# Gated cross-attention and expert layer: query rows made and turned earlier in a block, a written-out prologue order, and W_qv loaded from ScalarE's queue

## The reference, cut to what matters

```python
x = x + tanh(g_x) * xattn(layernorm(x), ctx)          # x: 4096 x 512, ctx: 3202 x 512
x = x + tanh(g_f) * moe(layernorm(x))                 # 8 experts, top 2, 512 -> 2048 -> 512, gelu

def xattn(e, c):
    Sim = (e @ w1)[:, None] + (c @ w2)[None, :] + (e * w3) @ c.T + b
    hq = softmax(Sim, axis=1) @ c                     # each row of x looks at all of ctx
    hc = softmax(max(Sim, axis=1)) @ e                # one pooled row for all of x
    return concat([e, hq, e * hq, e * hc]) @ W_qv + b_qv
```

## Time and profile before

| | |
|---|---|
| median of 3 runs | 2383.6 us |
| the profiled execution | 2384.36 us |
| its span | 2382.6 us |
| granted TensorE clock, mean | 0.967 |
| TensorE busy | 2215.5 us (93%) |
| VectorE, ScalarE busy | 1304.1 us (55%), 1146.8 us (48%) |
| share of the chain of waits: TensorE, VectorE, DMA | 82%, 5%, 4% |

### The profile page before, as it was taken

How to read it: one execution, slowest core, us unless ns; L and a number is a source line. 1 busy time by engine, 2 the same in 40 slices (tenths; PEclk the granted TensorE clock), 3 DMA queues, 4 the chain that set the end, 5 groups by cost and what they waited for, 6 DMA issues and landing times.

```text
span 2382.6 us, 34706 instructions
## 1 busy us (share of the span) xinstructions
PE 2215.5 (93%) x12045; PEld 1134.6 (48%) x12045; DVE 1304.1 (55%) x2667; ACT 1146.8 (48%) x1749; POOL 143.9 (6%) x141
## 2 busy tenths in 40 slices
PE   4799999999999999999899998599999999999997
PEld 2344444444444444444444544365564656556463
DVE  5556555555554555554366677556464555646450
ACT  4655555455555455554453334354463635446360
POOL 0000000000000000000002221201011010101101
PEclk8999999999999999999999999799999999999999
DMA  6444433444443344433578774433334353333421
GB/s 186 100 95 103 97 98 75 96 100 103 94 97 77 95 101 95 100 82 77 136 223 221 214 193 124 117 100 88 101 88 110 140 129 97 93 101 88 115 75 22
DMA packets 480081, 264.81 MB, mean 111 GB/s; under 512 B 419380, under 2 KB 419508, under 8 KB 475948
## 3 DMA queue, kind: packets, MB, share of 16 engines
q1 hardware_dynamic: 469164, 243.85, 38.4%
q0 software_dynamic: 10880, 20.52, 4.5%
HBM read 97.96 MB, written 71.52 MB: 71 GB/s over the span
## 4 chain that ended last, share of the span: by engine, by line
PE 82%; DVE 5%; DMA 4%; ACT 3%; issue 2%; SPq 1%; another core or an unknown queue 1%; POOL 1%; DVEq 0%; POOLq 0%; ACTq 0%
PE ps L1178 22%; PE ps L1194 19%; PE ps L1828 18%; PE ps L1843 17%; PE ps L1578 4%; DMA arena<-arena 3%; DMA rows<-arena 1%; SPq L526 1%; PE ps L364 1%; ACT arena L1047 1%; DVE arena L766 1%; ACT arena L1026 1%; ACT arena L1036 0%; ACT arena L995 0%
## 5 line engine op out<-in xcount | busy, mean ns | idle before, releaser
L1178 PE MATMUL ps<-arena 128*128 128x512 f16 (+1 forms) x2688 | 591.1, 373 | 64.2 <-DMA arena<-arena 61.1
L1194 PE MATMUL ps<-arena 128*128 128x512 f16 x2400 | 557.4, 381 | 0.0
L1828 PE MATMUL ps<-arena 128*128 128x320 f16 x3072 | 420.1, 300 | 17.3 <-DMA arena<-rows 17.3
L1178 PEld LDWEIGHTS ps<-arena 128*128 128x128 f16 x2688 | 257.0, 101 | 369.3 <-issue 108.1
L1843 PE MATMUL ps<-arena 128*128 128x512 f16 x1920 | 415.7, 379 | 0.0
L1026 ACT ACTIVATE arena<-ps,arena 128x512 f32<-128x512 f32 (+1 forms) x224 | 163.8, 732 | 499.1 <-PE ps L1178 499.1
L1194 PEld LDWEIGHTS ps<-arena 128*128 128x128 f16 x2400 | 235.5, 99 | 282.1 <-issue 11.8
L1828 PEld LDWEIGHTS ps<-arena 128*128 128x128 f16 x3072 | 301.1, 98 | 136.1 <-issue 17.4
L753 DVE TENSOR_REDUCE arena<-arena 128x1 f32<-128x512 f32 (+1 forms) x224 | 140.3, 626 | 312.1 <-ACT arena L1026 311.4
L1843 PEld LDWEIGHTS ps<-arena 128*128 128x128 f16 x1920 | 187.9, 98 | 225.3
L766 DVE SCALAR_TENSOR_TENSOR arena<-arena 128x512 f16<-128x512 f32 x192 | 144.1, 750 | 184.2 <-ACT arena L1047 184.2
(11 more groups left out here) (230 smaller groups left out, 1380.5 us busy)
## 6 DMA issues: line engine op xcount, KB each, us to landing
arena<-in_L_ffn_w SPq DMA_DIRECT2D x64, 1024.0 KB, 9.9
feats<-arena SPq DMA_DIRECT2D x48, 512.0 KB, 2.8
arena<-in_x SPq DMA_DIRECT2D x32, 512.0 KB, 3.6
rows<-arena SPq DMA_DIRECT2D x13, 774.0 KB, 3.8
out<-arena SPq DMA_DIRECT2D x16, 512.0 KB, 2.9
arena<-in_ctx SPq DMA_DIRECT2D x6, 1024.0 KB, 13.2
arena<-arena SPq DMA_TRANSPOSE x272, 3.1
arena<-in_L_xattn_W_qv SPq DMA_DIRECT2D x4, 1024.0 KB, 10.1
```

The source lines that it names most:

```text
L1178: mm = pe.matmul(out, qT[:, q, s * KD + k, :], ctxT[:, r * KD + k, a:z], start=(k == 0 and s + r == 0), stop=(k == KD - 1 and s == 1))
L1194: mm = pe.matmul(psO[q], turned, ctxN[:, j, r, :], start=(j + s + r == 0), stop=False)
L1828: mm = pe.matmul(psH[:, f % 2, h, :], w1s[:, s, k * F + f * P:k * F + (f + 1) * P], XT[:, r, k, h * HALF:(h + 1) * HALF], start=(k + s + r ...
```

## The change

The query rows of both units of the next block are made at steps 0 and 3 of the second half, their high parts at steps 1 and 4, their low parts at steps 2 and 5. SyncE turns the even one behind the fourth transpose of P. In the prologue the loop over t is gone and each engine has its order written out. Context tiles 0 to 3 are turned by TensorE and the other 22 by DMA; VectorE makes all four copies of turned tiles. `FIRST[q][c]` is the place of unit q's chunk c in the common order of the first 14 score groups. The low part and the pooling weight of a block's normalised rows have semaphores of their own, and those of block 1 are made in `half(1, 0)`. At the hand-over ScalarE issues the four loads of W_qv, one behind each of the probabilities 0 to 3 of unit 31; all four sums stand at step 0 of the last half; and SyncE loads the first features and rows of x for the merge right behind the transposes of unit 31, ahead of the store of unit 30.

The diff, cut to its core; the long orders of the prologue are given as lists.

```diff
-    def load_weights(self, sp):
-        for n in range(4):
-            (the four W_qv parts, on sp)
+    def load_weights(self, eng, n):
+        (part n alone, on eng)
...
-    LAG = 3
-    BY_PE = list(range(2 * TC))
+    FIRST = ((0, 1, 2, 3, 5, 7, 8), (4, 6, 9, 10, 11, 12, 13))
-    LK = 5 * QT + 2
+    LK, EK = 3 * QT + 1, QT + 1
-    UNIT0 = LAG + 2 * (LAST - LAG) + 1
+    UNIT0 = FIRST[0][LAST] + 1
+    psQ = ps[:, 3, :].bitcast(F16).rearrange("p (k i) -> p k i", i=P)
...
 sync, body:
+                if c == 2 and first:
+                    store_e(1)
+            if last:
+                load_first()
             for c in range(NC):
                 if not last:
                     turn_p(u, c)
+                if c == 3 and norms:
+                    turn_q(u + 2, 0)
                 if c == 4:
                     store_f(u - 2, 0)
-                if c == 5 and norms:
-                    turn_q(u + 2, 0)
+        def load_first():
+            sp.wait_ge(qk_done, NC * U)
+            sp.wait_ge(e_out, 16 * NB)
+            for v in range(2):
+                sp.wait_ge(f_out[v], 16 * (U // 2))
+            mg.load_feats(sp, feats, 0, 0)
+            mg.load_x(sp, x, 0, 0)
+            sp.wait_ge(p_ready, NC * U)
+            mg.load_feats(sp, feats, 1, 1)
+            mg.load_x(sp, x, 1, 1)
 sync, prologue:
+        for j in range(TC, JT):
+            turn_ctx(j)
+        load_x(2)
         turn_q(2, 0)
+        store_e(0)
         for c in range(NC):
             turn_p(0, c)
-        store_e(1)
+        mg.load_small(sp)
         turn_q(3, 1)
 sync, end (the waits and loads that load_first() now has are gone from behind body(NB)):
-        sp.wait_ge(qk_done, NC * U)
-        mg.load_weights(sp)
+        sp.wait_ge(rows_blank, 16 * (NB - 2))
         body(NB, last=True, norms=False, loads=False)
...
 vector, half:
+                if norms and i and c in (2, 5):
+                    query_lo(2 * b + 2 + c // 3, c // 3, row0)
                 if c == 1 and not (first and not i):
                     outputs(u - 3, b - 1 if i else b + XR - 2, old)
...
-                if norms and i:
-                    if c in (2, 4):
-                        query_rows(2 * b + 2 + q, b + 1, q, row0, 0)
-                    if c in (3, 5):
-                        query_lo(2 * b + 2 + q, q, row0)
+                if first and not i:
+                    if c == 0:
+                        norm_lo(1)
+                    if c == 1:
+                        norm_weight(1)
+                if norms and i and c in (0, 3):
+                    query_rows(2 * b + 2 + c // 3, b + 1, c // 3, row0, 0)
...
 vector, prologue, in its new order (";" for a new line):
+ query_rows(0, 0, 0, ..); query_rows(0, 0, 1, ..); chunk_scale(0); ident; chunk_scale(1); split_low(0); split_low(1)
+ split_low(2); chunk_scale(2); turned(0); split_low(3); query_lo(0, ..); turned(1); split_low(4); turned(2)
+ chunk_scale(3); split_low(5); turned(3); split_low(6); split_low(7); chunk_scale(4); query_lo(1, ..); split_low(8)
+ split_low(9); chunk_scale(5); chunk_max(0, 0, 0); copy of qT[:, 1]; split_low(10); split_low(11); chunk_max(1, 0, 1)
+ chunk_scale(6); norm_stats(1); chunk_max(2, 0, 2); split_low(12); norm(1); query_rows(2, ..); common_scale()
+ chunk_max(3, 0, 3); query_lo(2, ..); chunk_max(4, 1, 0); norm_lo(0); chunk_max(5, 0, 4); (6, 1, 1); (7, 0, 5); (8, 0, 6)
+ row_max(0, ..); low(0, 0, 0); chunk_max(9, 1, 2); low(0, 0, 1); chunk_max(10, 1, 3); low(0, 0, 2); chunk_max(11, 1, 4)
+ low(0, 0, 3); query_rows(3, ..); chunk_max(12, 1, 5); low(0, 0, 4); chunk_max(13, 1, 6); row_max(1, ..); low(0, 0, 5)
+ query_lo(3, ..); low(0, 0, 6); norm_weight(0); pool_top(0, ..); tail_low(); value_scale(); pool_rows(0, ..)
 scalar, half:
-                if norms and i and c in (3, 5):
-                    query_high(2 * b + 2 + q, q, row0, RK * (2 * b + 2 + q) + 2)
+                if norms and i and c in (1, 4):
+                    query_high(2 * b + 2 + c // 3, c // 3, row0, RK * (2 * b + 2 + c // 3) + 2)
+                if last and not i and c < 4:
+                    if c == 0:
+                        act.wait_ge(qk_done, NC * U)
+                    mg.load_weights(act, c)
-                if last and i and c < 4:
-                    mg.sum_part(act, c)
+                if last and i and c == 0:
+                    for n in range(4):
+                        mg.sum_part(act, n)
+                if first and not i and c == 0:
+                    norm_hi(1)
 scalar, prologue, in its new order (scores(n) is the evacuation of the n-th group):
+ squares(0); query_high(0, ..); squares(1); split_high(0); squares(2); split_high(1); (2); (3); squares(3)
+ split_high(4); (5); squares(4); copy of qT[:, 0]; split_high(6); (7); squares(5); query_high(1, ..); scores(0)
+ split_high(8); (9); squares(6); scores(1); split_high(10); (11); scores(2); norm_sd(1); scores(3); split_high(12)
+ scores(4); query_high(2, ..); scores(5); scores(6); norm_hi(0); scores(7); scores(8); scores(9); wait common
+ probabilities 0, 1; scores(10); probabilities 2; scores(11); 3; scores(12); 4; scores(13); 5; query_high(3, ..); 6; pool_weight(0)
 tensor, prologue, in its new order (first_scores(q, c) waits for ct_turned[c] and the bank, then scores):
+ sums(0); sums(1); sums(2); turn(0); turn(1); sums(3); turn(2); turn_query(0, psQ); turn(3); sums(4); wait q0_ready, ct_out
+ first_scores(0, 0); (0, 1); sums(5); (0, 2); turn_query(1, psT[0]); sums(6); (0, 3); (1, 0); (0, 4); (1, 1); (0, 5); (0, 6)
+ (1, 2); (1, 3); wait common, g_step; psV; (1, 4); (1, 5); (1, 6)
```

More of the change, by code:

```diff
@@ L951, in vector @@
[L951 to L963 removed]
+        split_low(2)
+        chunk_scale(2)
@@ new lines, in vector @@
+        turned(0)
+        split_low(3)
+        query_lo(0, 0, rowbuf[0])
+        turned(1)
+        split_low(4)
+        turned(2)
+        chunk_scale(3)
+        split_low(5)
+        turned(3)
+        split_low(6)
+        split_low(7)
+        chunk_scale(4)
+        query_lo(1, 1, rowbuf[1])
+        split_low(8)
+        split_low(9)
+        chunk_scale(5)
+        chunk_max(FIRST[0][0], 0, 0)
+        dve.wait_ge(q0_done, 2)
+        dve.tensor_copy(qT[:, 1], psT[0]).then_inc(q0_ready, 1)
@@ L1130, in scalar @@
-        act.wait_ge(common, 4)
-        for c in range(NC):
-            probabilities(0, 0, c)
-            if c == 0:
-                query_high(3, 1, row0, RK * 3 + 2)
-            if c + LAST - LAG + 1 < NC:
-                n = UNIT0 + 1 + c
-                scores(n, n % 4, 1, c + LAST - LAG + 1)
-            if c == 1:
-                pool_weight(0)
+        squares(1)
+        split_high(0)
+        squares(2)
+        split_high(1)
+        split_high(2)
+        split_high(3)
+        squares(3)
@@ new lines, in scalar @@
+        split_high(4)
+        split_high(5)
+        squares(4)
+        act.wait_ge(q0_done, 1)
+        act.copy(qT[:, 0], psQ).then_inc(q0_ready, 1)
+        split_high(6)
+        split_high(7)
+        squares(5)
+        query_high(1, 1, rowbuf[1], 4)
+        scores(FIRST[0][0], 0, 0, 0)
+        split_high(8)
+        split_high(9)
+        squares(6)
+        scores(FIRST[0][1], 1, 0, 1)
+        split_high(10)
+        split_high(11)
+        scores(FIRST[0][2], 2, 0, 2)
+        norm_sd(1)
@@ L1140, in scalar @@
+        scores(FIRST[1][4], 3, 1, 4)
+        probabilities(0, 0, 3)
+        scores(FIRST[1][5], 0, 1, 5)
+        probabilities(0, 0, 4)
+        scores(FIRST[1][6], 1, 1, 6)
+        probabilities(0, 0, 5)
+        query_high(3, 1, row0, RK * 3 + 2)
+        probabilities(0, 0, 6)
+        pool_weight(0)
         half(1, 0, first=True)
@@ L1252, in tensor @@
         pe.matmul(psV, vmax.broadcast_to([P, P]), identf, start=True, stop=True).then_inc(v_done, 1)
-        for c in range(LAST - LAG + 1, NC):
-            n = UNIT0 + c - LAG
-            pe.wait_ge(scores_ready, n - 3)
-            scores(n % 4, 1, c)
+        first_scores(1, 4)
+        first_scores(1, 5)
+        first_scores(1, 6)
         half(1, 0, first=True)
```

270 lines of the change are left out of this document (114 added, 156 removed).

## The result

The changed kernel takes 2266.64 us (median of 4 runs, 2265.27 to 2268.44) against 2383.43 us (4 runs, 2383.19 to 2384.3) of the kernel before on the same chip: a ratio of 0.951, 95% interval 0.9493 to 0.9526. The forecast was 2259.0, in a range of 2248 to 2280. The table shows one step that is 9.1 us off, the hand-over, and all others within 1.1 us.

What follows compares the result with a forecast made beforehand. TensorE was taken as busy nearly everywhere, with room only in prologue, blocks and hand-over; gains of 29, 88.1 and 7.5 us, 124.6 in all, took the profiled 2384.36 us to 2259.8, as median 2259.0, range 2248 to 2280.

Steps and rivals of the forecast that it cites:

- Part 1: Blocks: query rows at step 0, even tile turned at step 3, closes TensorE's hole at each block border; 88.1 us.
- C: Block border: the hole closes but a next wait of 1 to 2 us shows; 2280 us, chance 0.07.
- D: Blocks: query row not ready by step 3, SyncE stands at it, 88.1 us stay; 2347 us, chance 0.03.
- E: Blocks: without rests TensorE is granted the low clock for part of them, so slower; 2560 us, chance 0.02.
- Part 2: Prologue: squares and splits up to three groups ahead of the scores break a one-behind-the-other chain; 29 us.
- The walk: Prologue: new engine orders stepped forward with old durations; steady start at 71 to 73 us instead of 103.7.
- Part 3: Hand-over to the merge: W_qv loads from ScalarE's queue let P's transposes land in 5 to 8 us; 7.5 us.
- sign of being wrong: Hand-over: a merge that starts 48 us after the last scores, as before the change.
- Rival A: Hand-over: W_qv's packets take the transposes' place on the DMA engines, only issue time gained, 2.4 us; 2264.1 us, chance 0.2.
- the sum: Whole kernel: gains of 88.1, 29 and 7.5 us off the profiled execution's 2384.36 us give 2259.8 us.

Runs made afterwards that it cites:

- e1: Changed kernel with the even query tile's transpose back behind P's sixth transpose, rows still made at steps 0 and 3: 2353.27 us.
- e2: Changed kernel with the query rows made at their old steps, the even tile's transpose still behind P's fourth: 2263.62 us.
- e8: Kernel before, with TensorE's sums in the prologue's loop moved behind the first score group of each step: 2376.84 us.
- e12: Kernel before, with the prologue's scales, squares, sums and splits one chunk further ahead and sums behind scores: 2367.36 us.
- e7: Changed kernel with norm_sd(1) behind split_high(12) and the thirteenth evacuation ahead of the fourth probability on ScalarE in the prologue: 2266.62 us.
- e10: Changed kernel run once more, nothing changed: 2261.5 us.
- e3: Changed kernel with the four W_qv loads on SyncE's queue ahead of the last unit's transposes of P, as before the change: 2262.0 us.
- e11: Changed kernel with all four W_qv loads issued by ScalarE at once behind probability 0: 2259.35 us.
- after: First run of the changed kernel as it stands, against the kernel before: 2266.64 us, ratio 0.951.
- e5: Changed kernel with the W_qv loads on SyncE's queue behind all seven transposes of the last unit: 2267.81 us.
- e6: Changed kernel with one W_qv load on SyncE behind each of the last unit's transposes 1 to 4, sums between the last probabilities: 2261.5 us.

## Why the prediction was right, and where it was not

**Part 1 was right in size and mechanism.** 88.0 us for 88.1, blocks at clock 1.00. By e1, 89.8 us are lost again when one DMA goes back to its old place in SyncE's order. What I had put beside it as its condition, the row made at step 0, is none (e2): the row at step 2 was early enough. Rivals C and D, a next wait at the border or a row too late, are not there, and E, the lower clock, neither.

**Part 2 was right in size:** 30.0 us for 29. The walk said that half (1,0) would start at 71.3, and it started at 72.21, with the slow first group that it allowed for. That squares, splits and sums ran one behind the other was a part of the cause: breaking it in one place gives 8.1 us (e8), looking ahead in all three gives half (e12), and where the other half comes from is open. Two things were read or argued wrongly. The period of 10.75 us does not hold for each chunk: the groups of scores start at 44.55, 55.30 and 66.05, and from there on TensorE has two and more groups in a row. And the walk has a stall of 4 us at norm_sd(1) on the way; moving it, together with one evacuation, gained nothing that can be told from the spread of the other runs (e7). So the 30.0 us agree with the walk's 29 better than its account of them does.

**Part 3 was the term that failed.** The step was "I expect the first transposes to take 5 to 8 us instead of 3.1, the sums to start at 1192 to 1194". They took 11.47 us, and again 9.99; the sums started 31.8 us after the last scores, not 22 to 24, and the stage became 1.6 us longer instead of 7.5 shorter (0.5 shorter in e10, and 1.0 shorter to 0.5 longer in e1, e2 and e7). The sign of being wrong that the prediction gave, a merge 48 us after the last scores, came true. I had taken the other queue to let the transpose pass a part of the loads. e3, e10 and e11 show that this gains nothing: the transpose lands about when the loads under way do, on either queue. That only two loads are out at the first transpose is right, and in e1, e2, e7 and e10 it takes 7.9 to 8.3 us, at the upper end of the 5 to 8. But the other two are then issued at the very moment of release, and a second pair of transposes meets them (its first one takes 9.99 to 11.46 us in the five profiles). That second meeting is what the term left out. Rival A, with 2264.1, was nearest to the 2266.6; its mechanism is right for the transfers, and it too missed the second meeting. The range held because it took in rival A and because parts 1 and 2 came out; a hand-over worth nothing was not forecast. Part 3 is off by 7.5 + 1.6 = 9.1 us; with -1.0 of part 2, 0.1 of part 1, -0.7 of the later stages and 0.2 around the span that makes the 7.7 us between the profiled execution's 2267.52 and the sum's 2259.8.

On the pages: the Trainium skill (DMA: Bandwidth & Descriptors, section "Issuing engines are not separate DMA queues") says that transfers interleave whichever engine issued them, and that a second issuer saves only issuing time. The runs agree in kind: 47.2 us with SyncE's queue (e3), 45.8 with ScalarE's at once (e11), 1.4 us apart for an issue of 2.19 us. The section "Queues, rings and completion order" of the same page of the Trainium skill has the engines change between queues packet by packet, by which I had hoped for a share. The trace of e11 agrees: 1155 packets of the transposes beside 1165 of the loads. It is a share by packets, and with 256 B against 2 KB it is a ninth of the bytes, so the transpose was still 4.8 to 8.4 us late for 5.4 us of transfer. Why after's first transpose took 3 us more than those of the four other profiles, no run here tells.

## What to carry to other kernels

Where a wait stands once a block, find the queue on which the awaited transfer is issued and what is in front of it: one line moved in SyncE's order was worth 88 of 117 us. A large load moved to another engine's queue still holds up a small latency-bound transfer by about its own length, and spreading it in time can make two meetings of one. Put the load where lateness of the small transfers is hidden (one behind each), then look for the next bound, since three chains end close together here: P's transposes, the loads with their sums, and TensorE's pooled rows.

## What was not expected of the hardware

- A DMA transpose of 3.05 us takes 7.9 to 11.5 us with 2 MB of loads under way on another queue (after, e1, e2, e7, e10), and 11.9 to 13.6 us with 4 MB, on either queue (e11; e3 and the earlier trace rows). The same order of work gave 11.47 us in one profile and 7.88 to 8.31 in four others.
- Beside loads on the other queue, transposes and loads move packets one for one: 1155 of 256 B beside 1165 of 2 KB in 7 us (e11).
- 1 MB loads land every 2.7 us when four are queued, some 390 GB/s, but the first one took 5.9 us (e5). One in front of each transpose makes that transpose take 4.7 to 6.5 us (e6), which costs ScalarE no wait there.
- TensorE behind 3.09 us of idleness takes 4.17 us for a group of 2.75 (after), behind 1.35 us of it 2.75 (e7).
